# The last sequence's second half in its own banks: where the tail of one transformer layer is computed and sent

## The chip, the cores and the metric

The kernel runs on one NeuronCore of a Trainium2 chip. The metric is the device time of one execution in microseconds (us); the time of a version is the median over several executions. TensorE, VectorE, ScalarE, GpSimd (POOL) and SyncE each have a queue of their own and are ordered only by semaphores.

## The reference

One layer over 16 sequences of 256 tokens and 128 features: attention of 16 heads of 8 features with rotary positions and a causal mask, then a mixture of eight experts with one expert for each token, each followed by a residual addition and a normalisation.

```python
x = _layernorm(x + attention(x, wq, bq, wk, bk, wv, bv, wo, bo))
x = _layernorm(x + ffn(x, wg, W, b))
# _layernorm(x) = (x - mean) / sqrt(var + 1e-5), over the 128 features
# ffn: probs = softmax(x @ wg), expert = argmax(probs); a token counts if fewer
#      than 512 tokens before it took the same expert; out = prob * (x @ W[e].T + b[e])
```

## The kernel before

The work is a software pipeline over sequences. A loop over steps s runs on every engine (all_steps); in step s the stages of several sequences stand side by side: n = s+2 (projections and rotation), a = s+1 and b = s (operands and row maxima of the scores), c = s-1 (scores, exponentials, product with V), d = s-2 (output projection, first norm, routing, experts) and e = s-3 (second norm and output). Each step has 14 numbered slots, and each engine's order in a step is written out by hand by slot. Steps go from -2 to B+1 = 17; with B = 16 sequences the last step, 17, holds only d = 15 and e = 14, and behind it comes a short epilogue for e = 15. In the last step and the epilogue there are no other sequences' scores beside the chain.

In a step, what bears on the change is this. TensorE: the output projection of d (line 900, into ps_n), transposes of x1 (906), routing logits (948), locations (956 to 962), and the experts in two halves of 128 tokens, t = 0 in slot 12 and t = 1 in slot 13 (function experts, lines 814 to 816 through three, and 834). A half writes two PSUM banks, ps_m, one for experts 0 to 3 and one for 4 to 7: four matmuls of 512 columns for each bank, eight in all. The fourth adds a large negative number to all experts but the chosen one, so that VectorE finds the token's output as a maximum over the eight experts (select, line 668, into y_sel). Half 1 waits in TensorE's queue for moe_taken, which select of half 0 increments, since both halves use ps_m.

VectorE: in slot 3 it takes the second half of sequence e (select), in slot 4 it makes z2 = y_sel * gate_kept + x1 of e (add_experts, line 661, one instruction a half) and behind that z1 = projection + x_bias of d (line 706) with its statistics (norm_stats, lines 649 and 653, into st1 and mv1), in slot 5 x1 of d (line 712, two instructions, one a half), in slot 11 the statistics of z2.

GpSimd: inverse_deviation (line 356 adds epsilon, line 358 raises to the power -0.5) turns mv1 into rs1 and mv2 into rs2. output(e) does that for the second norm, waits until the store before has landed, scales z2 into y_out (line 367, one instruction a half) and sends both halves as one DMA from its own queue (line 372, semaphore stored). At the end it waits for all 16 stores.

SyncE's queue issues the loads and the traffic of rotated parts through DRAM (plain_parts, line 323, 64 KB each). Its last DMA is the load of x_res of sequence 15 (line 315), which GpSimd adds to a bias into x_bias (line 400).

After the last step the epilogue is: on VectorE select(15, 1), add_experts(15), norm_stats of z2; on GpSimd output(15).

Of the kernel before, what the change touches and what calls it, by code (L numbers as in the profile page):

```python
# [27 lines left out]
B, S, D = 16, 256, 128  # L28
# [60 lines left out]
def layer_kernel(nc, x, wq, bq, wk, bk, wv, bv, wo, bo, wg, W, b, const, expert_rows, out):  # L89
    f32, fr, bf = mybir.dt.float32, mybir.dt.float32r, mybir.dt.bfloat16  # L90
    ALU, ACT, AX = mybir.AluOpType, mybir.ActivationFunctionType, mybir.AxisListType
    x_t = x.rearrange("b (n p) d -> b p n d", p=128)
    out_t = out.rearrange("b (n p) d -> b p n d", p=128)
# [4 lines left out]
    with ExitStack() as ctx:  # L98
# [3 lines left out]
        def pb(name, shape):  # L102
            return ctx.enter_context(nc.psum_tensor(name, shape, f32))
# [28 lines left out]
        route_rows = sb("route_rows", [128, E * 128], fr)  # L132
# [30 lines left out]
        x_res, x_bias = sb("x_res", [128, 2, 128]), sb("x_bias", [128, 2, 128])  # L163
# [11 lines left out]
        kept, n_kept, gate_kept = sb("kept", [128, 2, E]), sb("n_kept", [128, 2]), sb("gate_kept", [128, 2])  # L175
        route = sb("route", [128, S], fr)

        ps_a = [pb(f"ps_a{i}", [128, 512]) for i in range(2)]
        ps_b = [pb(f"ps_b{i}", [128, 512]) for i in range(2)]
        ps_pv = pb("ps_pv", [128, 2, S])  # L180
        ps_m = pb("ps_m", [128, 2, 512])
        ps_n = pb("ps_n", [128, 512])
# [5 lines left out]
        names = []  # L188
# [18 lines left out]
                    gate_done rank_done first_done chosen_done seen_done loc_ready route_done nkept_done gk_done  # L207
                    moe_ready moe_taken""".split()

        names += """z2_done st2_done mv2_done ve2_done rs2_done out_done""".split()  # L210
        s_ = {name: sem(name) for name in names}

        def after(eng, name, t, per=1, k=0):

            n = t * per + k
            if isinstance(n, int):
                n = min(n, B * per)
                if n <= 0:
                    return
            eng.wait_ge(s_[name], n)  # L220
# [5 lines left out]
        def of_seq(v, t):  # L226

            return v[t] if isinstance(t, int) else v[bass.ds(t, 1)].squeeze(0)
# [18 lines left out]
        def by_half(t):  # L247

            return t[:, :, :].rearrange("p j (half m) -> p j half m", half=2)

        def is_step(s, which):

            return isinstance(s, int) and s == which

        def has(t):
            return not isinstance(t, int) or 0 <= t < B
# [9 lines left out]
        def all_steps(eng, step):  # L266


            for s in range(-2, 3):
                step(s, s % 2, lambda o: (s + o) // 2)  # L270
            with eng.Fori(0, (B - 6) // 2) as u:
                for k in range(2):
                    step(u * 2 + (3 + k), (3 + k) % 2, lambda o: u + (3 + k + o) // 2)
            for s in range(B - 3, B + 2):
                step(s, s % 2, lambda o: (s + o) // 2)
# [5 lines left out]
        def _(sp):  # L281
# [64 lines left out]
                    load_b(b, p)  # L346

            all_steps(sp, step)

        @block.gpsimd  # L350
        def _(pool):
# [8 lines left out]
            def output(e):  # L360

                inverse_deviation(mv2, rs2, 2, e)
                after(pool, "rs2_done", e, 1, 1)
                after(pool, "stored", e, 16)
                pool.nop(nofuse=True)
                for t in range(2):
                    last = pool.tensor_scalar(y_out[:, t, :], z2[:, t, :], mv2[:, t, 0:1], rs2[:, t:t + 1],  # L367
                                              ALU.subtract, ALU.mult)
                last.then_inc(s_["out_done"], 1)
                after(pool, "out_done", e, 1, 1)  # L370
                pool.nop(nofuse=True)
                pool.dma_start(of_seq(out_t, e), y_out[:, :, :]).then_inc(s_["stored"], 16)
# [87 lines left out]
                    output(e)  # L460

            all_steps(pool, step)
            output(B - 1)
            pool.wait_ge(s_["stored"], 16 * B)

        @block.scalar
        def _(act):
# [100 lines left out]
        def _(dve):  # L568
# [76 lines left out]
            def norm_stats(z, st, mv, n, d):  # L645

                after(dve, f"z{n}_done", d, 1, 1)
                for t in range(2):
                    dve.bn_stats(st[:, t, :], z[:, t, :]).then_inc(s_[f"st{n}_done"], 1)
                for t in range(2):  # L650
                    after(dve, f"st{n}_done", d, 2, t + 1)
                    dve.nop(nofuse=True)
                    dve.bn_aggr(mv[:, t, :], st[:, t, :]).then_inc(s_[f"mv{n}_done"], 1)  # L653

            def add_experts(e):

                after(dve, "out_done", e)
                for t in range(2):
                    after(dve, "moe_taken", e, 2, t + 1)
                    after(dve, "gk_done", e, 1, 1)  # L660
                    last = dve.scalar_tensor_tensor(out=z2[:, t, :], in0=y_sel[:, t, :], scalar=gate_kept[:, t:t + 1],
                                                    in1=x1[:, t, :], op0=ALU.mult, op1=ALU.add)
                last.then_inc(s_["z2_done"], 1)

            def select(d, t):

                after(dve, "moe_ready", d, 2, t + 1)
                dve.tensor_reduce(y_sel[:, t, :], ps_m[:, :, :].rearrange("p a (e f) -> p f (a e)", e=4),  # L668
                                  AX.X, ALU.max).then_inc(s_["moe_taken"], 1)

            def step(s, p, half):
                n, a, b, c, d, e = s + 2, s + 1, s, s - 1, s - 2, s - 3
                for slot in range(SLOTS):
# [21 lines left out]
                    if slot == 2 and has(d):  # L695
# [1 line left out]
                        after(dve, "y_ready", d)  # L697
                        after(dve, "den_done", d, 2, 2)
                        dve.tensor_tensor(attn[:, :], weighted[:, :], inv_den[:, :], ALU.mult).then_inc(s_["normed"], 1)
                    if slot == 4 and has(e):  # L700
                        add_experts(e)
                    if slot == 4 and has(d):

                        after(dve, "y_ready", d, 1, 1)
# [2 lines left out]
                                          x_bias[:, :, :], ALU.add).then_inc(s_["z1_done"], 1)  # L707
                        norm_stats(z1, st1, mv1, 1, d)
                    if slot == 5 and has(d):
                        after(dve, "rs1_done", d, 1, 1)  # L710
                        for t in range(2):
                            dve.tensor_scalar(x1[:, t, :], z1[:, t, :], mv1[:, t, 0:1], rs1[:, t:t + 1],  # L712
                                              ALU.subtract, ALU.mult).then_inc(s_["x1_done"], 1)
# [63 lines left out]

            all_steps(dve, step)
            select(B - 1, 1)
            add_experts(B - 1)  # L780
            norm_stats(z2, st2, mv2, 2, B - 1)

        @block.tensor
        def _(pe):
# [33 lines left out]
            def experts(d, n, t):  # L818

                if t == 0:  # L820
                    if has(n):
                        after(pe, "roped", n, 1, 1)
                    else:
                        after(pe, "vrows_done", d + 2, 1, 1)
                else:
                    after(pe, "moe_taken", d, 2, 1)
                for h in range(2):
                    o = ps_m[:, h, :].rearrange("p (e f) -> p e f", e=4)
                    tok = slice(128 * t, 128 * t + 128)
                    three(o, (x1t_hi[:, tok], x1t_lo[:, tok]), (we_hi[:, 4 * h:4 * h + 4, :], we_lo[:, 4 * h:4 * h + 4, :]),  # L830
                          True, False)
                    if h == 0:
                        after(pe, "route_done", d, 1, 1)
                    mm = pe.matmul(ps_m[:, h, :], route[:, tok], route_rows[:, 512 * h:512 * h + 512],  # L834
                                   start=False, stop=True, skip_group_check=True)
                mm.then_inc(s_["moe_ready"], 1)

# [181 lines left out]
```

## Time and profile before

| what | us |
|---|---|
| three runs | 463.35, 462.91, 461.01 |
| median | 462.91 |
| the profiled execution, its own time | 461.8 |
| its span in the trace | 460.1 |
| TensorE busy in the span | 410.3 |

The span goes from the first to the last instruction of the core; the execution's own time is 1.7 us more. The granted TensorE clock was 0.971 of full in the mean. The rows below are from that execution, and their times count from the span's start. The names PE, PEld, DVE, ACT, POOL and SP are TensorE's matmuls, its weight loads, VectorE, ScalarE, GpSimd and SyncE; a q behind a name is the engine's queue or sequencer. In the chain of waits, a piece begins where the piece before it released it, so that an instruction's piece can be shorter than the instruction. "issue" is time in which an engine waited for nothing that the profile shows.

### The profile page before, as it was taken

The numbers are of one execution on the slowest core, as the hardware profiler recorded it, in microseconds if no ns is written. First come the engines' busy times: TensorE is split into PE (matmuls) and PEld (weight loads), VectorE is DVE, ScalarE is ACT, GpSimd is POOL, SyncE is SP. The second block draws the span as 40 slices with busy tenths as digits, with TensorE's granted clock in tenths as the row PEclk, the third lists the DMA queues.
The fourth block names the chain that finished last, engine by engine and source line by source line (L and its number), as shares of the span: only waits on it lengthen the run. The fifth ranks groups of instructions, "written<-read, shape, count | busy, mean of one in ns | idle before, by whom it ended". The sixth has DMA issues, their size and how long they took to land. (4 is left out here: it accounts for less than half of the span.)

```text
span 460.1 us, 10441 instructions
## 1 busy us (share of the span) xinstructions
PE 410.3 (89%) x3270; PEld 359.2 (78%) x3270; DVE 317.8 (69%) x809; ACT 170.4 (37%) x375; POOL 207.8 (45%) x384
## 2 busy tenths in 40 slices
PE   3548598999999999999999999999999999999651
PEld 2426497989899888989898989898989888988540
DVE  8395444668686877877787878786868686855542
ACT  5152234343343434433434343434344343344100
POOL 6562324342545455463646463636363545151333
PEclk9999798999999999999999999999999999999957
DMA  5299872857669594939393939496678677610000
GB/s 139 51 156 157 131 111 61 134 88 133 95 122 123 122 115 113 130 93 151 84 160 88 147 84 144 90 147 92 144 99 147 82 134 97 76 33 1 11 0 24
DMA packets 145587, 47.29 MB, mean 103 GB/s; under 512 B 104333, under 2 KB 141841, under 8 KB 145562
## 3 DMA queue, kind: packets, MB, share of 16 engines
q1 hardware_dynamic: 139610, 42.52, 58.2%
q10 hardware_dynamic: 5184, 2.36, 2.7%
q0 software_dynamic: 768, 2.10, 1.6%
q8 instruction: 13, 0.21, 0.2%
q14 instruction: 12, 0.10, 0.1%
HBM read 30.70 MB, written 14.68 MB: 99 GB/s over the span
## 5 line engine op out<-in xcount | busy, mean ns | idle before, releaser
L881 PE MATMUL ps_pv<-probs,v_diag 128*128 128x64 f32 (+3 forms) x1024 | 190.0, 321 | 3.1 <-ACT probs L517 2.7
L881 PEld LDWEIGHTS ps_pv<-probs,v_diag 128*128 128x128 f32 x1024 | 148.0, 192 | 12.0 <-ACT probs L517 6.2
L517 ACT ACTIVATE probs<-ps_b 128x512 f32<-128x512 f32 (+1 forms) x176 | 97.5, 559 | 149.3 <-PE ps_b L845 145.0
L682 DVE TENSOR_REDUCE row_max<-ps_a 128x2 f32<-128x512 f32 (+3 forms) x176 | 108.3, 631 | 22.3 <-PE ps_a L845 21.9
L869 PE MATMUL ps_a<-k_plain,q_diag 128*128 128x64 bf16 (+3 forms) x512 | 67.2, 242 | 7.7 <-DMA q_diag<-plain_parts 4.4
L860 PE MATMUL ps_b<-q_plain,k_diag 128*128 128x64 bf16 (+3 forms) x512 | 65.6, 236 | 3.4 <-DMA q_plain<-max_rows 3.4
L668 DVE TENSOR_REDUCE y_sel<-ps_m 128x128 f32<-128x1024 f32 x32 | 39.0, 1219 | 18.7 <-PE ps_m L834 18.7
L869 PEld LDWEIGHTS ps_a<-k_plain,q_diag 128*128 128x128 bf16 x512 | 35.1, 101 | 20.2 <-issue 8.6
L419 POOL COPY v_diag<-v_rows 64x128 f32<-64x128 f32 x64 | 18.4, 288 | 68.6 <-PE ps_pv L881 33.9
L860 PEld LDWEIGHTS ps_b<-q_plain,k_diag 128*128 128x128 bf16 x512 | 36.3, 98 | 11.5 <-issue 4.2
L845 PE MATMUL ps_a<-mask_a_bf,ident_bf 128*128 128x128 bf16 (+2 forms) x176 | 44.6, 254 | 0.0
L845 PE MATMUL ps_b<-mask_b_bf,ident_bf 128*128 128x128 bf16 (+2 forms) x176 | 43.3, 246 | 0.0
L692 DVE RECIPROCAL inv_den<-sums 128x128 f32<-128x128 f32 x16 | 15.2, 953 | 37.0 <-ACT sums L483 37.0
L356 POOL TENSOR_SCALAR rs<-mv 128x2 f32<-128x2 f32 x32 | 7.3, 229 | 73.4 <-DVE mv L653 73.4
L451 POOL TENSOR_TENSOR rot_rest<-rot 128x512 f32<-128x512 f32 x16 | 18.5, 1154 | 38.0 <-ACT rot L561 38.0
L814 PE MATMUL ps_m<-we_hi,x1t_hi 128*128 128x512 f32 x64 | 28.6, 448 | 1.3 <-DVE y_sel L668 1.3
L753 DVE SCALAR_TENSOR_TENSOR rot_cs<-ps_m,bias_cols,cst 128x256 f32<-128x256 f32 x32 | 15.3, 479 | 19.5 <-PE ps_m L816 19.5
L448 POOL TENSOR_TENSOR rot<-rot_cs 128x512 f32<-128x512 f32 x16 | 20.6, 1288 | 14.2 <-DVE rot_cs L756 12.5
L367 POOL TENSOR_SCALAR y_out<-z,mv,rs 128x128 f32<-128x128 f32 x32 | 25.4, 797 | 3.6 <-POOL rs L358 3.6
L815 PE MATMUL ps_m<-we_lo,x1t_hi 128*128 128x512 f32 x64 | 25.8, 403 | 0.0
L816 PE MATMUL ps_m<-we_hi,x1t_lo 128*128 128x512 f32 x64 | 25.7, 402 | 0.0
L834 PE MATMUL ps_m<-route_rows,route 128*128 128x512 f32 x64 | 25.5, 399 | 0.0
(142 smaller groups left out, 716.3 us busy)
## 6 DMA issues: line engine op xcount, KB each, us to landing
plain_parts<-rot SPq DMA_DIRECT2D x180, 64.0 KB, 2.0
k_plain<-plain_parts SPq DMA_DIRECT2D x16, 384.0 KB, 3.8
q_diag<-plain_parts SPq DMA_DIRECT2D x32, 192.0 KB, 5.3
q_plain<-plain_parts SPq DMA_DIRECT2D x16, 384.0 KB, 6.2
k_diag<-plain_parts SPq DMA_DIRECT2D x32, 192.0 KB, 6.6
x_in<-in_L_attn_x_dram SPq DMA_DIRECT2D x16, 128.0 KB, 5.9
x_res<-in_L_attn_x_dram SPq DMA_DIRECT2D x16, 128.0 KB, 3.0
out_dram<-y_out POOLq DMA_DIRECT2D x16, 128.0 KB, 2.5
```

Of the source, the lines that this page charges most:

```text
L367: last = pool.tensor_scalar(y_out[:, t, :], z2[:, t, :], mv2[:, t, 0:1], rs2[:, t:t + 1], ALU.subtract, ALU.mult)
L517: act.activation(probs[:, k % PR, 0:cols], ps_b[k % 2][:, 0:cols], ACT.Exp, scale=SCALE)\
L668: dve.tensor_reduce(y_sel[:, t, :], ps_m[:, :, :].rearrange("p a (e f) -> p f (a e)", e=4), AX.X, ALU.max).then_inc(s_["moe_taken"], 1)
L682: last = dve.tensor_reduce(row_max[:, NBLK - 1 - j, groups[0]:groups[-1] + 1], scores[:, :, col:col + width(j)], AX.X, ALU.max)
L814: pe.matmul(out, sh, mh, start=start, stop=False, skip_group_check=True)
L815: pe.matmul(out, sh, ml, start=False, stop=False, skip_group_check=True)
L816: return pe.matmul(out, sl, mh, start=False, stop=stop, skip_group_check=True)
L834: mm = pe.matmul(ps_m[:, h, :], route[:, tok], route_rows[:, 512 * h:512 * h + 512], start=False, stop=True, skip_group_check=True)
L845: return pe.matmul(v, ident_bf[:, :], rows, start=False, stop=True, skip_group_check=True)
L860: pe.matmul(ps_b[k % 2][:, col:col + width(j)], diag_block(k_diag[q], g, j), q_plain[q][:, g, BLK * j:S], start=(i == 0), stop=False, skip ...
L869: pe.matmul(ps_a[k % 2][:, col:col + width(j)], diag_block(q_diag[at], g, NBLK - 1 - j), k_plain[at][:, g, 0:width(j)], start=(i == 0), st ...
L881: mm = pe.matmul(ps_pv[:, g // 4, BLK * j:S], v_diag[q][:, j, 128 * g:128 * g + 128], probs[:, k % PR, col:col + width(j)], start=(j == 0 ...
```

## The change

Only the last sequences are treated differently; the loop is as it was. The scores' four PSUM banks become one tensor ps_ab, cut into ps_a and ps_b as before. For sequence 15 the second half of the experts goes to the first two of these banks (expert_bank) and no longer waits for moe_taken. In step 17 the two additions of sequence 14 move from slot 4 to slot 5, behind z1 and its statistics, and x1 of sequence 15 waits for them, since they read x1 of sequence 14. For sequence 15 the second norm uses z1, st1, mv1 and rs1 in place of z2, st2, mv2 and rs2, and doesn't wait for the output of sequence 14. VectorE in place of GpSimd scales, from z1 into x_bias, one half at a time, and SyncE sends each half when it is done. GpSimd at the end waits for 15 stores and the two halves.

```diff
--- before.py
+++ after.py
@@ -175,8 +175,8 @@
         kept, n_kept, gate_kept = sb("kept", [128, 2, E]), sb("n_kept", [128, 2]), sb("gate_kept", [128, 2])
         route = sb("route", [128, S], fr)
 
-        ps_a = [pb(f"ps_a{i}", [128, 512]) for i in range(2)]
-        ps_b = [pb(f"ps_b{i}", [128, 512]) for i in range(2)]
+        ps_ab = pb("ps_ab", [128, 4, 512])
+        ps_a, ps_b = [ps_ab[:, i, :] for i in range(2)], [ps_ab[:, i, :] for i in range(2, 4)]
         ps_pv = pb("ps_pv", [128, 2, S])
         ps_m = pb("ps_m", [128, 2, 512])
         ps_n = pb("ps_n", [128, 512])
@@ -207,7 +207,7 @@
                     gate_done rank_done first_done chosen_done seen_done loc_ready route_done nkept_done gk_done
                     moe_ready moe_taken""".split()
 
-        names += """z2_done st2_done mv2_done ve2_done rs2_done out_done""".split()
+        names += """z2_done st2_done mv2_done ve2_done rs2_done out_done last_done last_stored""".split()
         s_ = {name: sem(name) for name in names}
 
         def after(eng, name, t, per=1, k=0):
@@ -247,6 +247,10 @@
         def by_half(t):
 
             return t[:, :, :].rearrange("p j (half m) -> p j half m", half=2)
+
+        def expert_bank(d, t):
+
+            return ps_ab[:, 0:2, :] if t == 1 and is_step(d, B - 1) else ps_m
 
         def is_step(s, which):
 
@@ -346,6 +350,10 @@
                     load_b(b, p)
 
             all_steps(sp, step)
+            for t in range(2):
+                sp.wait_ge(s_["last_done"], t + 1)
+                sp.nop(nofuse=True)
+                sp.dma_start(of_seq(out_t, B - 1)[:, t, :], x_bias[:, t, :]).then_inc(s_["last_stored"], 16)
 
         @block.gpsimd
         def _(pool):
@@ -460,8 +468,9 @@
                     output(e)
 
             all_steps(pool, step)
-            output(B - 1)
-            pool.wait_ge(s_["stored"], 16 * B)
+            inverse_deviation(mv1, rs1, 2, B - 1)
+            pool.wait_ge(s_["stored"], 16 * (B - 1))
+            pool.wait_ge(s_["last_stored"], 2 * 16)
 
         @block.scalar
         def _(act):
@@ -652,9 +661,10 @@
                     dve.nop(nofuse=True)
                     dve.bn_aggr(mv[:, t, :], st[:, t, :]).then_inc(s_[f"mv{n}_done"], 1)
 
-            def add_experts(e):
-
-                after(dve, "out_done", e)
+            def add_experts(e, z2):
+
+                if z2 is not z1:
+                    after(dve, "out_done", e)
                 for t in range(2):
                     after(dve, "moe_taken", e, 2, t + 1)
                     after(dve, "gk_done", e, 1, 1)
@@ -665,7 +675,7 @@
             def select(d, t):
 
                 after(dve, "moe_ready", d, 2, t + 1)
-                dve.tensor_reduce(y_sel[:, t, :], ps_m[:, :, :].rearrange("p a (e f) -> p f (a e)", e=4),
+                dve.tensor_reduce(y_sel[:, t, :], expert_bank(d, t)[:, :, :].rearrange("p a (e f) -> p f (a e)", e=4),
                                   AX.X, ALU.max).then_inc(s_["moe_taken"], 1)
 
             def step(s, p, half):
@@ -697,8 +707,8 @@
                         after(dve, "y_ready", d)
                         after(dve, "den_done", d, 2, 2)
                         dve.tensor_tensor(attn[:, :], weighted[:, :], inv_den[:, :], ALU.mult).then_inc(s_["normed"], 1)
-                    if slot == 4 and has(e):
-                        add_experts(e)
+                    if slot == (5 if is_step(s, B + 1) else 4) and has(e):
+                        add_experts(e, z2)
                     if slot == 4 and has(d):
 
                         after(dve, "y_ready", d, 1, 1)
@@ -707,6 +717,8 @@
                                           x_bias[:, :, :], ALU.add).then_inc(s_["z1_done"], 1)
                         norm_stats(z1, st1, mv1, 1, d)
                     if slot == 5 and has(d):
+                        if is_step(s, B + 1):
+                            after(dve, "z2_done", e, 1, 1)
                         after(dve, "rs1_done", d, 1, 1)
                         for t in range(2):
                             dve.tensor_scalar(x1[:, t, :], z1[:, t, :], mv1[:, t, 0:1], rs1[:, t:t + 1],
@@ -777,8 +789,12 @@
 
             all_steps(dve, step)
             select(B - 1, 1)
-            add_experts(B - 1)
-            norm_stats(z2, st2, mv2, 2, B - 1)
+            add_experts(B - 1, z1)
+            norm_stats(z1, st1, mv1, 2, B - 1)
+            after(dve, "rs2_done", B - 1, 1, 1)
+            for t in range(2):
+                dve.tensor_scalar(x_bias[:, t, :], z1[:, t, :], mv1[:, t, 0:1], rs1[:, t:t + 1],
+                                  ALU.subtract, ALU.mult).then_inc(s_["last_done"], 1)
 
         @block.tensor
         def _(pe):
@@ -822,16 +838,16 @@
                         after(pe, "roped", n, 1, 1)
                     else:
                         after(pe, "vrows_done", d + 2, 1, 1)
-                else:
+                elif not is_step(d, B - 1):
                     after(pe, "moe_taken", d, 2, 1)
                 for h in range(2):
-                    o = ps_m[:, h, :].rearrange("p (e f) -> p e f", e=4)
+                    o = expert_bank(d, t)[:, h, :].rearrange("p (e f) -> p e f", e=4)
                     tok = slice(128 * t, 128 * t + 128)
                     three(o, (x1t_hi[:, tok], x1t_lo[:, tok]), (we_hi[:, 4 * h:4 * h + 4, :], we_lo[:, 4 * h:4 * h + 4, :]),
                           True, False)
                     if h == 0:
                         after(pe, "route_done", d, 1, 1)
-                    mm = pe.matmul(ps_m[:, h, :], route[:, tok], route_rows[:, 512 * h:512 * h + 512],
+                    mm = pe.matmul(expert_bank(d, t)[:, h, :], route[:, tok], route_rows[:, 512 * h:512 * h + 512],
                                    start=False, stop=True, skip_group_check=True)
                 mm.then_inc(s_["moe_ready"], 1)
```

## Rows read from the trace of the kernel before

**Rows 1.** The page, engines: busy us, share of the span, instructions.

```profile
PE 410.3 (89%) x3270; PEld 359.2 (78%) x3270; DVE 317.8 (69%) x809; ACT 170.4 (37%) x375; POOL 207.8 (45%) x384
```

**Rows 2.** Stretches of ten us: busy of each engine, granted clock, DMA.

```profile
420.00:430.00 10.00, 9.99 (x88) 9.12 (x87) 4.52 (x19) 3.15 (x7) 3.50 (x7) 1.00 0.01 2
430.00:440.00 10.00, 3.84 (x19) 2.56 (x18) 5.97 (x14) 1.90 (x5) 1.93 (x4) 0.84 0.04 13
```

**Rows 3.** Chain of waits, 430 to 461 us: start us, length us, what.

```profile
433.46 1.22 DVE y_sel L668
...
435.20 0.34 DVE z L706
...
436.16 0.19 DVE mv L653
...
436.51 0.24 POOL rs L356
...
436.82 0.73 POOL rs L358
...
437.57 0.61 DVE x L712 x2
...
442.97 0.43 PE ps_m L814
...
445.95 0.44 PE ps_m L834
...
446.42 1.23 DVE y_sel L668
...
447.70 0.50 PE ps_m L814
448.19 0.23 PE ps_m L815
...
449.58 0.25 PE ps_m L834
...
452.88 0.73 POOL rs L358
...
453.81 1.59 POOL y_out L367 x2
...
455.94 0.82 POOL out_dram L372
```

**Rows 4.** TensorE in half-us stretches: length, busy, granted clock, DMA share, GB/s.

```profile
436.50:437.00 0.50, 0.00 (x0) 0.78 0.00 0
...
447.00:447.50 0.50, 0.00 (x0) 0.98 0.00 0
```

**Rows 5.** Line 774: duration ns min/median/max, first and last start.

```profile
L774 DVE TENSOR_TENSOR gate_kept<-n_kept,gate x16: 160/644/727, 93.9 to 443.7; 128x2 f32<-128x2 f32 x16
```

**Rows 6.** Timeline around 336 us: start us, length us, engine, line, what.

```profile
336.07 1.28 POOL L448 TENSOR_TENSOR rot<-rot_cs 128x512 f32<-128x512 f32 x1 [0.16 <-POOL seen L444]
...
336.65 0.71 DVE L774 TENSOR_TENSOR gate_kept<-n_kept,gate 128x2 f32<-128x2 f32 x1
```

**Rows 7.** DMA issues from 450 us on: KB, us from issue to landing.

```profile
out_dram<-y_out POOLq DMA_DIRECT2D x1, 128.0 KB, 2.4
```

**Rows 8.** Line 315's loads from 380 us on: issue ns, us to landing.

```profile
L315 SPq DMA_DIRECT2D x_res<-in_L_attn_x_dram x3: 390/2805/3222, 379.2 to 411.3; - x3
...
DMA to landing us min/median/max: 2.2/6.6/6.7
```

**Rows 9.** Line 323's writes to DRAM, whole trace: issue ns, us to landing.

```profile
L323 SPq DMA_DIRECT2D plain_parts<-rot x180: 539/547/937, 19.7 to 371.2; - x180
...
DMA to landing us min/median/max: 2.0/2.0/3.3
```

**Rows 10.** GpSimd's sequencer at the end of the program (L98), ns.

```profile
L98 POOLq DRAIN  x1: 1382/1382/1382, 458.5 to 458.5; - x1
```

**Rows 11.** GpSimd's sequencer at the start of the program (L1006), ns.

```profile
L1006 POOLq DRAIN  x1: 169/169/169, 0.4 to 0.4; - x1
```

## Prediction

> **What bounds the kernel now.** I read the page first. TensorE is busy 89% of the span [rows 1], so over the body of the kernel a change must relieve TensorE. The edits all lie in the last steps, so next I read the stretches of ten us: TensorE is full until 430 us and then falls to 38% [rows 2]. From there on it is one sequence's chain of dependent small steps. The third view, the chain of waits, is the one that prices this change. The reader is to see that from 433.46 us on it runs through every operation that the diff touches: the reduction of sequence 14's second half, its two additions, the normalisation of sequence 15, both halves of its experts, and the tail with inverse deviation, scaling and store [rows 3]. Whatever is taken out of this chain moves the end one for one, as long as nothing else becomes late. The fourth view is the granted clock in half-us stretches, since the second part of the change puts matmuls where TensorE now idles at half clock [rows 4].
>
> **Part 1, the two additions of sequence 14 go behind sequence 15's first norm.** At present VectorE ends the reduction at 434.68 and starts z1 at 435.20; between them stand the two additions of line 661, 0.52 us [rows 3]. The matmuls that z1 reads were done (the chain runs through the reduction, not through them), so z1 and all behind it could come 0.52 us earlier. The additions go between the norm statistics and x1. There VectorE now waits from 436.35 to 437.57 for the two GpSimd operations, lines 356 and 358 (starts 436.51 and 436.82) [rows 3]: 1.2 us of cover for 0.6 us of work. The added wait of x1 on z2_done holds nothing else back, for x1 is next in that queue anyway.
>
> But the cover is not free. Nowhere in the trace do the additions lie beside a GpSimd operation. The nearest row is line 774, a tiny product with both inputs in SBUF: it takes 0.16 us alone and 0.64 in the median, and in the instance shown it starts at 336.65 inside GpSimd's line 448 (336.07 for 1.28, to 337.35) and ends at 337.36 [rows 5, 6]. Such a VectorE operation stands still until GpSimd's is over. The additions have both inputs in SBUF too. They would start at once, 0.13 us or so before line 356, so here GpSimd may be the one that waits. Bounds: no collision, gain 0.52; GpSimd waits for both additions, or the second addition waits for line 358 and x1 for it, gain 0. I take 0.25, half way, since the collision is there [rows 6], but with the other engine first.
> The Trainium skill's page "SBUF — State Buffer", section "SBUF: two separate sides", says that VectorE with two SBUF inputs and GpSimd take a shared port pair in turn, whole instruction by whole instruction. The trace agrees [rows 6]. By that rule the gain of this part is near the low bound, by the cover alone at the high one; part 2 shows that the sum would be 0.14 us smaller or larger.
>
> **Part 2, the second half of the experts in other banks.** Now: the first half's eight matmuls stream from 442.97 to 446.39, 0.43 us apart; the reduction runs from 446.42 to 447.65; only then the second half starts at 447.70 and ends at 449.83, its matmuls 0.23 apart ((449.58 - 448.19)/6) after a first of 0.50 [rows 3]. With its own banks it starts right behind the first half. Only 1.31 us of idle time (446.39 to 447.70) and 0.27 of first-matmul fill can go. The 0.43 and 0.23 are the two levels of the clock: it fell to half (1.2 GHz) at about 436.8, when TensorE was mostly idle [rows 2], and was back at full (2.4 GHz) just after 447.0, behind the 3.4 us of the first half and during the wait for the reduction [rows 4]. So part of the second half now falls into the slow stretch. With part 1's 0.25, the stream starts at 442.72. A slow matmul takes (446.39 - 442.97)/8 = 0.4275. Up to 447.0, 4.28/0.4275 = 10.0 are done; the other 6.0 at 0.2325 take 1.39; end 448.39, against 449.83: 1.44 us for parts 1 and 2 together. Bounds: full clock from the first matmul of the second half, 446.14 + 8 x 0.2325 = 448.00, gain 1.83; half clock throughout, 446.14 + 8 x 0.4275 = 449.56, gain 0.27. With part 1 at its own bounds these become 2.1 and 0, and the middle case 1.58 (stream from 442.45) and 1.30 (from 442.97): of a shift ahead of the clock's rise only about half arrives behind it. I take the middle case, 1.44, as the rise stands there in the profile.
> The reduction of the first half (446.17 to 447.4) is then hidden behind the second half's matmuls, and the second reduction is not held up by it. It reads another pair of banks of the same size: 1.22 us as before. The last users of those banks, the maxima of sequence 15, come before its scores are exponentiated, long before 433, so that this wait costs nothing.
> The Trainium skill's page "TensorE: Matmul & The Clock Gate", section "Part 1: The HAM clock gate", says that activity releases the slower clock, and that the moment varies from run to run. The trace agrees on the two levels [rows 4]. By that rule the 1.44 is one draw out of the cases between the bounds.
>
> **Part 3, from the last matmul to the inverse deviation.** Same operations on z1, st1, mv1, rs1 in place of z2, st2, mv2, rs2. The chain from 449.83 to 453.61 stays: 3.78 us [rows 3], 0. Dropping the wait on out_done gives nothing: GpSimd's scaling of sequence 14 does not stand in the chain, the additions follow the reduction.
>
> **Part 4, scaling and store.** Now, counted from the end of rs (453.61): scaling starts at +0.20 and takes 1.59 on GpSimd, the DMA issue starts at +2.33 [rows 3] and the data land 2.4 later [rows 7], at 458.3 or +4.7. After: VectorE starts 0.03 after rs, two scalings in 0.61, as line 712 does on the same shape [rows 3]; the first is done at +0.37, SyncE issues at about +0.45. SyncE's queue is empty: its last DMA was the load of x_res at 411.3 [rows 8]. An issue of 64 KB from there costs 0.55 us, up to 0.94 [rows 9], so the second goes out at about +1.1, although its data is there at +0.64. Landing of 64 KB written to DRAM from SyncE: 2.0 in the median of 180, 3.3 at most [rows 9]. End at +3.1, against +4.7: gain 1.6. Bounds: issue 0.39, the least of the loads of x_res [rows 8], gain 1.8; landing 3.3, gain 0.3. The landing on an idle queue is the median's case, so I take 1.6. The tail of sequence 15 needs no more of GpSimd than lines 356 and 358.
> What follows the landing stays: GpSimd waits for last_stored in place of stored, then its DRAIN of 1.38 us (458.5 to 459.87) ends the span [rows 10]. That is the largest unpriced item. At the start of the span a DRAIN of GpSimd took 0.17 [rows 11], with no DMA of GpSimd's before it. After the change its last own DMA lies 9 us back. Bounds: 0 and -1.2; I take 0, since the DMA had landed before the DRAIN began in this trace also.
>
> **The sum.** 1.44 + 0 + 1.6 = 3.0 us. The profiled execution took 461.8 with a span of 460.1, so 458.8 with a span of 457.1. That execution lies 1.1 below the median of the three runs (462.91, from 461.01 to 463.35); the four average 462.3, which gives 459.3, and that is the forecast. A difference of 0.5% (2.3 us) is about what a measurement of this kernel can tell from none, and the forecast is not far beyond it. The rest of the kernel, up to 433 us, keeps the same instructions and the same banks: ps_a and ps_b are now one tensor cut in four.
>
> **The rivals.**
> A. The clock stays low through most of the second half. For: with no pause it starts 1.5 us sooner, nearer to the cold stretch. Against: more activity. Gain 0.27 + 1.6 = 1.9, time 460.4. Chance 0.17.
> B. The collision of part 1 eats all of it: line 356 begins behind both additions, at about 436.5 as now. For: the standstill of line 774 [rows 6]. Against: it is GpSimd that would have to stand, and short operations can take turns. Gain 1.30 + 1.6 = 2.9, time 459.4. Chance 0.15. (The page on SBUF named above would have it so.)
> C. GpSimd's closing DRAIN shrinks to 0.17. Gain 3.0 + 1.2 = 4.2, time 458.1. For: the start's DRAIN; against: above. Chance 0.12.
> D. The store in halves is no faster: a landing of 3.3 leaves 1.44 + 0.3 = 1.7, time 460.6. Chance 0.08.
> E. Slower: SyncE's queue gives late landings. Line 315, on the same queue, landed after 6.7 us at worst [rows 8]. Then the end is at +1.1 + 6.7 = +7.8 in place of +4.7, 3.1 lost, 1.44 won: 1.7 slower, 464.0. It decides from a landing of 5.0 us on. Against: those loads shared the queue with others' packets, and in the tail the DMA engines are nearly idle [rows 2]. Chance 0.04.
> F. The change does not do what it says: z1 or the second half is held by something that I don't see, and the net gain is under 1 us; 461.8. Chance 0.07.
>
> **How the numbers follow.** The forecast keeps 0.37. Faster by over 0.5%: forecast, B and C, 0.64, and a little of A and D by the spread of runs, 0.67. Within 0.5%: A, D and F, less that, 0.28. Slower: 0.05. The range takes in C below (458.1, less half a us for the spread) and A and D above, with the same allowance: 457.6 to 461.2. The likeliest case's own range is 458.4 to 460.0.
>
> **What would show it.** In the changed profile: z1 (line 706's successor) right behind the reduction, and the starts and durations of lines 356, 358 and 661 beside each other; sixteen expert matmuls without a gap, with the clock's rise somewhere in them and the last one's end some 1.4 us sooner; the second reduction starting at that end; two scalings of 0.34 on VectorE, two SyncE issues 0.6 apart, landing 2.0 after the second; GpSimd's DRAIN at 1.38. The prediction is wrong if the clock rises later than the end of the first half plus 2 us, if lines 356 and 358 start later than their cover allows, if landing takes over 3 us, or if the DRAIN changes.

## The result and the profile after

| | runs | median us | ratio to the kernel before |
|---|---|---|---|
| before | 4 | 462.54 (461.01 to 463.35) | |
| changed | 4 | 457.11 (456.55 to 457.47) | 0.9885 (0.9857 to 0.9914) |
| changed, measured again | 6 | 457.14 (456.32 to 459.51) | 0.9907 (0.9883 to 0.9932) |

The change wins 5.4 us where 3.0 to 3.2 were forecast, and ends half a us below the range. The profiled execution took 457.05 with a span of 455.4, so the two spans differ by 4.7. The second measurement gives 4.7 as well (461.87 for 19 executions of before). The ratios come from all executions of both kernels and differ a little from those of the medians. By the intervals of the ratios the gain lies between 4.0 and 6.6 us in the first measurement and between 3.1 and 5.4 in the second, so the first excludes the forecast 3.2 and the second has it at its edge.

The chain of waits of the changed kernel, in the tail (start us, length us, what). Lines 678, 716, 830, 832, 850, 366 and 796 answer to 668, 706, 814, 816, 834, 358 and 367 of [rows 3]:

```profile
433.17 1.22 DVE y_sel L678
434.38 0.34 DVE z L716
...
436.76 0.02 DVEq L220
...
442.22 0.43 PE ps_m L830
...
444.78 0.39 PE ps_m L832
445.17 0.24 PE ps_m L850
445.41 0.23 PE ps_ab L830
...
447.02 0.25 PE ps_ab L850
...
450.33 0.73 POOL rs L366
...
451.09 0.34 DVE x_bias L796
```

The reader sees z1 (434.38) right behind the reduction, the second half's matmuls (ps_ab, from 445.41) right behind the first half's, and the scaling (451.09) 0.03 us behind the inverse deviation. The granted clock of that trace in half-us stretches, as [rows 4]:

```profile
434.50:435.00 0.50, 0.00 (x0) 0.75 0.00 0
...
445.00:445.50 0.50, 0.50 (x4) 1.00 0.00 0
```

It fell at about 434.75 and rose at 445.0, within the first half: the seventh matmul of that half is the last slow one, and the whole second half runs at 0.23 us a matmul.

The timeline of the additions in their new place and of the last stores, then the stores' landing (KB, us from issue) and GpSimd's closing DRAIN, which answer to [rows 7] and [rows 10]:

```profile
435.48 0.61 DVE L671 SCALAR_TENSOR_TENSOR z<-y_sel,gate_kept,x 128x128 f32<-128x128 f32 x2
435.69 0.23 POOL L364 TENSOR_SCALAR rs<-mv 128x2 f32<-128x2 f32 x1 [4.98 <-DVE mv L662]
436.00 0.72 POOL L366 TENSOR_TENSOR rs<-rs,minus_half 128x2 f32<-128x2 f32 x1
...
451.09 0.60 DVE L796 TENSOR_SCALAR x_bias<-z,mv,rs 128x128 f32<-128x128 f32 x2 [1.24 <-POOL rs L366]
451.50 0.84 SPq L356 DMA_DIRECT2D out_dram<-x_bias  x2
```

```profile
out_dram<-x_bias SPq DMA_DIRECT2D x2, 64.0 KB, 1.6
```

```profile
L98 POOLq DRAIN  x1: 1301/1301/1301, 453.8 to 453.8; - x1
```

The two additions (line 671) and the two GpSimd operations behind the statistics lie side by side, none late or long against [rows 3]. Line 364 falls wholly inside the additions, line 366 overlaps them by only 0.09 us. The two stores take 0.84 us to issue, 0.37 each and a gap. With both traces cut at the same five places, the stages are, in us:

| stage | before | changed | won | forecast |
|---|---|---|---|---|
| body, up to the reduction of sequence 14 | 433.46 | 433.17 | 0.29 | 0 |
| from there to the first matmul of the experts | 9.51 | 9.05 | 0.46 | 0.25 |
| the experts' sixteen matmuls with the pause | 6.86 | 5.05 | 1.81 | 1.19 |
| last matmul to the end of the inverse deviation | 3.78 | 3.79 | 0 | 0 |
| from there to GpSimd's DRAIN | 4.9 | 2.8 | 2.1 | 1.6 |
| DRAIN to the end | 1.6 | 1.5 | 0.1 | 0 |

Of the 0.53 us by which z1 comes earlier, 0.46 reach the experts: x1 starts 0.10 us behind line 366 in place of 0.02, because VectorE passes the added wait on z2_done there (DVEq, line 220, above).

### The profile page after: what moved, and what is told of

Same layout as the page of the kernel before. It is cut to its first block and busy times, and to the rows that moved or that the text cites. A ratio compares the mean times of both kernels' runs of the same rounds, so it can differ in the third digit from the quotient of the medians.

```text
span 455.4 us, 10444 instructions
## 1 busy us (share of the span) xinstructions
PE 407.5 (89%) x3270; PEld 357.4 (78%) x3270; DVE 318.7 (70%) x811; ACT 170.4 (37%) x375; POOL 205.4 (45%) x381
## 5 line engine op out<-in xcount | busy, mean ns | idle before, releaser
L526 ACT ACTIVATE probs<-ps_ab 128x512 f32<-128x512 f32 (+1 forms) x176 | 97.5, 559 | 151.5 <-PE ps_ab L861 147.6
L692 DVE TENSOR_REDUCE row_max<-ps_ab 128x2 f32<-128x512 f32 (+3 forms) x176 | 108.4, 631 | 24.6 <-PE ps_ab L861 24.2
L885 PE MATMUL ps_ab<-k_plain,q_diag 128*128 128x64 bf16 (+3 forms) x512 | 67.7, 244 | 10.2 <-DMA q_diag<-plain_parts 5.0
L876 PE MATMUL ps_ab<-q_plain,k_diag 128*128 128x64 bf16 (+3 forms) x512 | 65.6, 236 | 2.8 <-DMA q_plain<-max_rows 2.8
L885 PEld LDWEIGHTS ps_ab<-k_plain,q_diag 128*128 128x128 bf16 x512 | 35.2, 101 | 22.9 <-issue 12.5
L678 DVE TENSOR_REDUCE y_sel<-ps_m 128x128 f32<-128x1024 f32 x31 | 37.8, 1220 | 16.2 <-PE ps_m L850 16.2
L876 PEld LDWEIGHTS ps_ab<-q_plain,k_diag 128*128 128x128 bf16 x512 | 36.3, 99 | 11.0 <-issue 3.7
L861 PE MATMUL ps_ab<-mask_a_bf,ident_bf 128*128 128x128 bf16 (+2 forms) x176 | 44.7, 254 | 0.0
L861 PE MATMUL ps_ab<-mask_b_bf,ident_bf 128*128 128x128 bf16 (+2 forms) x176 | 43.3, 246 | 0.0
L375 POOL TENSOR_SCALAR y_out<-z,mv,rs 128x128 f32<-128x128 f32 x30 | 23.7, 795 | 3.4 <-POOL rs L366 3.4
```

Of the source, the lines that this page charges most:

```text
L526: act.activation(probs[:, k % PR, 0:cols], ps_b[k % 2][:, 0:cols], ACT.Exp, scale=SCALE)\
L678: dve.tensor_reduce(y_sel[:, t, :], expert_bank(d, t)[:, :, :].rearrange("p a (e f) -> p f (a e)", e=4), AX.X, ALU.max).then_inc(s_["moe_t ...
L692: last = dve.tensor_reduce(row_max[:, NBLK - 1 - j, groups[0]:groups[-1] + 1], scores[:, :, col:col + width(j)], AX.X, ALU.max)
L861: return pe.matmul(v, ident_bf[:, :], rows, start=False, stop=True, skip_group_check=True)
L876: pe.matmul(ps_b[k % 2][:, col:col + width(j)], diag_block(k_diag[q], g, j), q_plain[q][:, g, BLK * j:S], start=(i == 0), stop=False, skip ...
L885: pe.matmul(ps_a[k % 2][:, col:col + width(j)], diag_block(q_diag[at], g, NBLK - 1 - j), k_plain[at][:, g, 0:width(j)], start=(i == 0), st ...
```

## The experiments

The stages of the profiled executions, worked out from their chains of waits in the same way (us; the body is left out, as it differs between executions of the same kernel):

| kernel | to the experts | experts | inverse deviation to DRAIN |
|---|---|---|---|
| before, first profile | 9.51 | 6.86 | 4.9 |
| before, second profile | 9.50 | 8.53 | 4.9 |
| additions alone | 9.05 | 8.41 | 4.9 |
| banks alone | 9.51 | 4.83 | 4.9 |
| tail alone | 9.51 | 8.53 | 2.8 |
| changed | 9.05 | 5.05 | 2.8 |
| changed, again | 8.82 | 4.98 | 2.8 |
| changed, with four additions | 9.20 | 5.81 | 2.8 |
| changed, with one store | 9.06 | 5.01 | 2.8 |
| before with fillers | 9.13 | 5.94 | 4.9 |
| changed with fillers | 8.18 | 3.88 | 2.8 |
| changed with more fillers | 8.18 | 3.89 | 2.8 |

In the second profile of the changed kernel the clock fell only at 437.4, in place of 434.75, so the two transposes of x1 took 0.47 us and not 0.70; hence its 8.82.

**1. The additions alone.**

```diff
-                    if slot == 4 and has(e):
+                    if slot == (5 if is_step(s, B + 1) else 4) and has(e):
                         add_experts(e)
...
                     if slot == 5 and has(d):
+                        if is_step(s, B + 1):
+                            after(dve, "z2_done", e, 1, 1)
```

> Only the two additions of sequence 14 are moved behind sequence 15's statistics; banks and tail are those of the kernel before. Theory 1 (no collision: the two engines' reads do not meet): z1 starts right behind the reduction, lines 356 and 358 keep their distance to the statistics and their 0.23 and 0.72 us, the time falls by 0.45 to 0.5 us. Theory 2 (shared port, as the prediction took half of it): line 356 or 358 is late or long, gain 0 to 0.25.

Measured: 461.38 (459.68 to 464.68, 12 runs), ratio 1.000 (0.9974 to 1.0026). An effect of 0.5 us is inside that interval, so the time can't confirm it; the trace does. Four of the twelve executions, the profiled one among them, took 464.1 to 464.7, above all 59 of before (463.9 at most), and the others 459.7 to 461.7. In the profiled one the reduction of sequence 14 came late, at 434.75, ahead of the edit's place; why is not shown. Its chain of waits:

```profile
434.75 1.22 DVE y_sel L668
435.96 0.34 DVE z L706
...
443.80 0.43 PE ps_m L816
...
448.53 0.80 PE ps_m L816
449.33 0.43 PE ps_m L817
```

From the reduction to z1 it is 1.21 us in place of 1.74, to the experts' first matmul 9.05 in place of 9.51: theory 1. But the second half (from 448.53) is at 0.43 us a matmul, and the experts take 8.41 in place of 6.86. The edit isn't needed for that: experiment 4 finds the same in the kernel before.

**2. The banks alone.** The edit is ps_ab, expert_bank and the wait on moe_taken, as in the change.

> Only the second half of sequence 15's experts goes to other banks. Theory 1 (the pause is what is won, the clock decides how much): no gap between the sixteen matmuls, gain 1.0 to 1.9 us, by where the clock rises: from the start of the first half to the end of the second 6.9 us before, 4.9 to 5.9 now. Theory 2 (without the pause the clock comes back reliably earlier, so the time of before had an additional loss in other executions): gain over 2 us in the median, and the spread of the runs is smaller than that of before.

Measured: 459.66 (457.31 to 460.70, 8 runs), ratio 0.9939 (0.9914 to 0.9964), 2.2 us in the medians. The chain of waits, where the clock rises and where the second half begins and ends:

```profile
443.91 0.43 PE ps_m L818
...
446.04 0.36 PE ps_m L819
...
446.87 0.23 PE ps_ab L818
...
448.49 0.25 PE ps_ab L838
```

Sixteen matmuls without a gap, 4.83 us: 2.03 less than in the first profile of before. The gain is over 2 us in the median, as theory 2 has it, but the interval (1.7 to 4.0) doesn't exclude theory 1, and the spread of the runs (3.4, of 8 executions) is hardly smaller than that of before (3.7, of 19). Which of the two is right stays open.

**3. The tail alone.** The change without expert_bank and without the move.

> Only the last norm's buffers, its scaling on VectorE and the store by SyncE in halves; additions and banks as before. Theory 1 (what the changed kernel's trace showed holds alone too): store lands 2.5 to 2.6 us after the inverse deviation in place of 4.7, gain 2.1 to 2.2 us. Theory 2 (the prediction's 1.6 was right for an ordinary landing and the trace had a lucky one): landing 2.0 after the issue, gain 1.6.

Measured: 459.65 (457.54 to 461.34, 6 runs), ratio 0.9937 (0.9913 to 0.9962), 2.2 us in the medians. The two stores and the DRAIN:

```profile
455.78 0.84 SPq L356 DMA_DIRECT2D out_dram<-x_bias  x2
```

```profile
L98 POOLq DRAIN  x1: 1301/1301/1301, 458.1 to 458.1; - x1
```

The inverse deviation ends at 455.33; the stores are issued and land as in the changed kernel (1.6 us), and it is 2.8 in place of 4.9 us to the DRAIN: theory 1.

All three parts together, once more:

> The changed kernel once more, beside the parts on the same chip. If the parts add, its gain is the sum of the three single gains within 0.5 us, 4.4 to 5.4 us. If one part opens room for another (the clock), it is more than the sum by over 0.5 us.

Measured: 457.14 (456.32 to 459.51, 6 runs), 4.7 us under before (461.87). The single gains are 0.5, 2.2 and 2.2 us by the medians, 4.9 together. By the medians the parts add. The ratios give 0, 2.8 and 2.9 us singly, 5.7 together, against 4.3 for the whole change, each with about 1.2 us to either side, so that the sum is known only within a us or two. That one part opens something for another is not seen.

**4. The kernel before, profiled once more.**

> The kernel before once more, for a second profile and more times. Theory 1 (in part of its executions the second half of the experts runs at half clock): the second half takes 3.4 us from the first reduction's start in some profiles and 5.0 to 5.1 in others; its times spread over 3 us or more. Theory 2 (both other kernels with the pause were slow by their own edits): 3.4 again, and a spread that comes from the body.

Measured: 461.07 (459.83 to 463.34, 10 runs), ratio 0.9994 (0.9972 to 1.0017). Its chain of waits, and its granted clock in half-us stretches:

```profile
433.01 1.22 DVE y_sel L668
...
442.51 0.43 PE ps_m L814
...
445.97 1.24 DVE y_sel L668
...
447.25 0.80 PE ps_m L814
448.04 0.43 PE ps_m L815
...
450.60 0.44 PE ps_m L834
...
451.07 0.07 DVE y_sel L668
```

```profile
446.50:447.00 0.50, 0.00 (x0) 0.50 0.00 0
...
451.00:451.50 0.50, 0.03 (x1) 0.88 0.00 0
```

The same kernel, but the clock rises at 451.1 in place of 447.0, and the second half (447.25 to 451.04) runs at 0.43 us a matmul. The experts take 8.53 us in place of 6.86. Theory 1: with the pause, the kernel before has both outcomes, 1.67 us apart. Its copies with the additions or the tail alone have one profile each, and both show the slow one (8.41 and 8.53); so of the four profiles with the pause three are slow, and the forecast was built on the fourth. How often each outcome comes can't be told from four. This execution took 463.0. In the profiles with the new banks the clock rose from 2.3 to 4.4 us behind the first matmul, so that the experts took 4.83 to 5.81 us and never the whole 6.8 of sixteen slow ones.

**5. The clock held up.** In step 17, matmuls of 512 columns that nobody reads go into TensorE's idle times: 13 behind the output projection, 2 behind the transposes, 5 behind the logits.

```diff
+            def fill(count):
+                for _ in range(count):
+                    pe.matmul(ps_ab[:, 3, :], ident_bf[:, :], q_plain[0][:, 0:2, :], start=True, stop=True,
+                              skip_group_check=True)
...
                         mm.then_inc(s_["y_ready"], 1)
+                        if is_step(s, B + 1):
+                            fill(13)
```

> The changed kernel with 20 matmuls of 512 columns more in step 17 (13 behind the output projection, 2 behind the transposes, 5 behind the logits) into an idle bank; nobody reads them. Theory 1 (the clock sets what is left of the experts' time): the granted clock stays at full from 433 us on, the first half's matmuls come 0.23 us apart in place of 0.43, the sixteen take 3.7 us in place of 5.1 to 5.3, transposes and logits are shorter too; the time falls by 1.5 to 2.5 us against the changed kernel. Theory 2 (the slow matmuls are slow for what they read, not for the clock): 0 or a loss, as the fillers stand in the queue ahead of the chain.

Measured: 454.42 (453.55 to 456.77, 6 runs), ratio to before 0.9838 (0.9808 to 0.9868), 7.9 us under before and beyond the interval of the changed kernel. No version that was run has a lower median. Five-us stretches of TensorE (busy, granted clock), and the chain of waits:

```profile
430.00:435.00 5.00, 3.64 (x19) 1.00 0.01 2
435.00:440.00 5.00, 3.58 (x18) 1.00 0.00 0
440.00:445.00 5.00, 4.34 (x21) 1.00 0.00 0
```

```profile
432.33 1.22 DVE y_sel L678
...
440.51 0.24 PE ps_m L830
...
441.21 0.38 PE ps_m L856
...
442.52 0.23 PE ps_ab L830
...
444.14 0.25 PE ps_ab L856
```

The clock is at 1.00 until the experts are done, and they take 3.88 us: all sixteen matmuls at full clock, with a wait of 0.15 us for the routing. Theory 1.

The kernel before with the same fillers:

> The kernel before with the same 20 matmuls. Theory 1: both halves run at full clock in every execution, 1.9 us each with the pause between, so that it wins 1.6 us (first half) against the profiled execution of before and up to 1.6 more against executions in which the second half was slow too: 2 to 3 us in the median. The difference between this kernel and the changed one with fillers is then what the clock has no part in: 0.5 for the additions, 1.3 + 0.3 for the pause, 2.15 for the tail, 4.2 us together. Theory 2: as for the other kernel, 0 or a loss.

Measured: 458.99 (457.64 to 459.29, 6 runs), ratio 0.9925 (0.9900 to 0.9950), 3.4 us under before. Its granted clock shows that 20 fillers don't always hold it:

```profile
439.00:439.50 0.50, 0.50 (x3) 0.69 0.00 0
...
442.50:443.00 0.50, 0.50 (x4) 0.90 0.00 0
```

It was low from 439.2 to 442.6, against theory 1, which had both halves at full clock in every execution. The five fillers behind the logits then ran slow as well: from the logits to the locations it was 1.87 us, where the changed kernel with fillers has 1.40. The experts still take 5.94 us, 0.9 to 2.6 less than without fillers. Against the changed kernel with fillers the difference is 4.6 us in the medians, where 4.2 were worked out.

The changed kernel with 27 fillers:

> As the changed kernel with fillers, with 27 of them (4 more ahead of the output projection, 14, 3 and 6 in the three other pauses). Theory 1 (the clock fell inside the tail in some executions with 20 fillers, as in the trace of the kernel before with fillers): fewer executions over 455.5 us, median at or up to 0.5 us below that with 20. Theory 2 (20 are enough, more only delay the chain): median 0.2 to 0.5 us higher.

Measured: 454.73 (453.39 to 455.54, 5 runs), ratio 0.9853 (0.9832 to 0.9873). The tail is as long as with 20 fillers (both 20.1 us from the reduction of sequence 14 to the end), and the medians can't be told apart; one execution of five was over 455.5 (455.54), where with 20 it was one of six (456.77). Which theory is right stays open.

**6. VectorE against GpSimd in the cover.** Two more additions of the same form stand ahead of the two moved ones.

```diff
+                        if is_step(s, B + 1):
+                            for t in range(2):
+                                dve.scalar_tensor_tensor(out=weighted[:, 128 * t:128 * t + 128], in0=y_sel[:, t, :],
+                                                         scalar=gate_kept[:, t:t + 1], in1=x1[:, t, :],
+                                                         op0=ALU.mult, op1=ALU.add)
                         add_experts(e, z2)
```

> The changed kernel with two more additions of the same form ahead of the two moved ones (into a buffer that nobody reads any more), so that VectorE works with two SBUF inputs during all of lines 356 and 358 of before (364 and 366 now). Theory 1 (no standstill at this size): the four start 0.26 to 0.27 us apart, the two GpSimd operations keep their starts at 0.16 and 0.47 after the statistics and their 0.23 and 0.72 us. Theory 2 (they take turns, and the two additions had only missed each other): one of the two engines is held, an addition lasts over 0.5 us or a GpSimd operation starts over 0.2 late, and x1 is later by as much as exceeds the cover.

Measured: 458.58 for one execution. Its timeline (start, length, engine, line), to be held against that of the changed kernel above:

```profile
436.05 0.58 DVE L713 SCALAR_TENSOR_TENSOR weighted<-y_sel,gate_kept,x 128x128 f32<-128x128 f32 x2
436.31 0.23 POOL L364 TENSOR_SCALAR rs<-mv 128x2 f32<-128x2 f32 x1 [4.99 <-DVE mv L662]
436.56 0.60 DVE L671 SCALAR_TENSOR_TENSOR z<-y_sel,gate_kept,x 128x128 f32<-128x128 f32 x2
436.62 0.86 POOL L366 TENSOR_TENSOR rs<-rs,minus_half 128x2 f32<-128x2 f32 x1
```

And line 671 alone:

```profile
L671 DVE SCALAR_TENSOR_TENSOR z<-y_sel,gate_kept,x x2: 339/340/340, 436.6 to 436.8; 128x128 f32<-128x128 f32 x2
```

With four, the additions keep their pace, line 364 its 0.23 us, and line 366 takes 0.86 in place of the 0.72 that it has again at 451.85 in the same execution. So there is a collision, but it costs GpSimd 0.14 us, with two more additions than the change has. Neither theory is right as put: no standstill, but one operation longer by a fifth. The last addition began at 436.8, inside line 366 (436.62 to 437.48), and took its 0.34 us all the same. So it isn't only that VectorE came first: here GpSimd's operation was under way, as line 448 was in [rows 6], and nothing stood still. That is one execution.

**7. What in the tail is won.** One store by SyncE behind both scalings:

```diff
-            for t in range(2):
-                sp.wait_ge(s_["last_done"], t + 1)
-                sp.nop(nofuse=True)
-                sp.dma_start(of_seq(out_t, B - 1)[:, t, :], x_bias[:, t, :]).then_inc(s_["last_stored"], 16)
+            sp.wait_ge(s_["last_done"], 2)
+            sp.nop(nofuse=True)
+            sp.dma_start(of_seq(out_t, B - 1), x_bias[:, :, :]).then_inc(s_["last_stored"], 16)
```

> The changed kernel with one store of 128 KB by SyncE behind both scalings in place of two. Theory 1 (the start on SyncE and the short landing are what is won, the halves hardly matter): the store is issued 0.7 us after the inverse deviation and lands after 1.7 to 1.9, so that the end is 0.1 us earlier to 0.1 later than with halves. Theory 2 (halves overlap): it lands 2.0 or more after its issue, the end is 0.2 to 0.4 later.

Measured: 457.62 for one execution. Timeline, and the landing:

```profile
450.87 0.72 POOL L365 TENSOR_TENSOR rs<-rs,minus_half 128x2 f32<-128x2 f32 x1
...
452.30 0.39 SPq L355 DMA_DIRECT2D out_dram<-x_bias  x1
```

```profile
out_dram<-x_bias SPq DMA_DIRECT2D x1, 128.0 KB, 1.9
```

The store is issued at +0.71 behind the inverse deviation (451.59) and lands 1.9 later; with halves the second is issued at +0.91 and lands 1.6 later. From the inverse deviation to the DRAIN it is 2.81 against 2.77 us: theory 1, the halves are worth nothing that one execution of each could show.

The same single store from GpSimd's queue, behind VectorE's scaling:

> The changed kernel, scaled by VectorE, but sent by GpSimd in one store of 128 KB. Theory 1 (scaling and queue each give a part): the issue comes 0.7 + 0.5 us after the inverse deviation (0.5 for GpSimd's start of a store, as in the kernel before), lands 2.3 to 2.4 later: store landed at +3.6, against +2.6 with SyncE and +4.7 before; so 1.1 of the 2.15 us is the scaling and 1.05 the queue. Theory 2 (GpSimd's lateness came from its own scaling just before): issue 0.1 after the scaling, landed at +3.1.

Measured: 457.95 for one execution. Timeline, and the landing:

```profile
450.25 0.72 POOL L362 TENSOR_TENSOR rs<-rs,minus_half 128x2 f32<-128x2 f32 x1
...
452.15 0.78 POOL L471 DMA_DIRECT2D out_dram<-x_bias  x1 [1.18 <-issue]
```

```profile
out_dram<-x_bias POOLq DMA_DIRECT2D x1, 128.0 KB, 2.3
```

Issued at +1.18, landed 2.3 later at +3.5, the DRAIN starts at +3.7. Of the 2.1 us, 1.2 come from the scaling on VectorE (4.9 to 3.7) and 0.9 from SyncE's queue (3.7 to 2.8). Theory 1.

## Why the prediction was wrong

The direction, the places and the order of the parts were right, and parts 1, 2 and 4 each gave more than their terms of the sum. The mechanism held; what failed were three sizes, and two of them, the experts and the store, were each short by about 0.6 us. Rivals A to F did not occur: the clock came back earlier, not later; the DRAIN took 1.30 us, not 0.17; and the stores landed early.

**Part 1** was sized at 0.25 and measured 0.53 up to z1, 0.46 up to the experts. The step that failed is the carrying over of line 774's standstill [rows 5, 6] to the additions. There the GpSimd operation ran over 512 elements for 1.28 us; lines 356 and 358 work on two. Experiment 6 gives 0.14 us as the cost of a longer overlap, and in the change itself nothing got longer, so the bound 0.52 was nearly the right value; the added wait, which the text put at nothing, costs the 0.07 between it and 0.46. Experiment 6 also rules out that only the order of the two engines differs. That GpSimd's small operand is what spares VectorE is argued, not shown. The trace agrees less with the Trainium skill's page "SBUF — State Buffer", section "SBUF: two separate sides", than I made it. In [rows 6] the standstill of line 774 shows as a longer record, 0.71 us in place of 0.16. By turns of whole instructions line 364, which began inside the first addition, or the second addition, which began inside line 364, would be long in the same way; they took 0.23 and 0.34 us, as alone. Whether the reads themselves take turns within these times is not shown.

**Part 2** was sized at 1.19 (1.44 with part 1) and measured 1.81. The step that failed is the middle case: it kept the rise of the clock at the profile's 447.0, 4.3 us behind the first matmul. In the changed kernel it came 2.8 us behind it (445.0 - 442.22), and over the profiles with new banks 2.3 to 4.4 behind: the last of these, with four additions, took 5.81 us, near the 5.67 of the forecast. It was a draw, as the text said, but the bounds were too narrow for it on both sides. On the side of the change, they let the clock rise with the first matmul of the second half at the earliest, which gives 2.1 us for parts 1 and 2 together. The measured 2.27 lie beyond, because the clock rose within the first half. On the side of before, they took the 6.86 us of its profile as the time to be beaten, and the second profile has 8.53. Between 8.53 and 5.05 the same edit wins 3.5 us. So a forecast from one profile of before could have been off by 1.7 us for this alone, and the range had no such term. That the measured stage came as near to the forecast as 0.6 us is in part luck: the profile of before happened to be the fast outcome.

**Part 3** was right: 3.79 us against 3.78, and dropping the wait on out_done gave nothing.

**Part 4** was sized at 1.6 and measured 2.1. Two durations of [rows 9] did not hold for this store: the issue took 0.37 us, not 0.55 (the lower bound 0.39 of [rows 8] was right), and the landing 1.6, although the least of the 180 was 2.0. The bounds of the landing came from one kind of write, and so there was none below 2.0. Why this store lands sooner than those writes is not shown. The DRAIN was right, 1.30 against 1.38, though GpSimd's own last store was 6 us back and not 9.

**The sum.** By stages the tail won 4.45 us in place of 3.0: 0.2 from part 1, 0.6 from part 2, 0.6 from part 4 with the DRAIN. The body gave another 0.29, which nothing in the change explains: over the traces of this case the reduction of sequence 14 starts anywhere from 432.2 to 434.8. The spans account for 4.7 of the 5.4; the rest comes of medians of four executions: the median of all 59 executions of before is 461.95, that of all ten of the changed kernel 457.11, 4.8 us. The first profile of before, at 461.8, was close to its kernel's median after all, and moving the forecast up by half a us towards 462.3 took it further from the measured time. What spreads the body's start and the times of before (459.7 to 463.9), beyond the 1.7 us of the experts, stays open.

## What to carry to other kernels

In a tail of dependent steps, add up the chain and then ask for each term whether its duration is a constant or a draw: here matmuls behind a quiet stretch took 0.23 or 0.43 us by the moment at which the clock rose, and one profile shows one draw. A pause in TensorE ahead of its last work can cost more than its own length: here it was 1.3 us long, and removing it won 2.2 by the medians. Matmuls that nobody reads, put into such pauses, won 2.7 us, at least as much as any single edit of the change. For a last output, the engine that scales and the queue that sends are each worth about a us; cutting the store in halves showed no gain.

## What the runs showed of the hardware

- The same kernel's second half ran at 0.23 us a matmul in one execution and at 0.43 in another, by a rise of the granted clock at 447.0 or 451.1.
- The first matmul behind the pause took 0.50 us at full clock and 0.80 at half clock, 0.27 and 0.37 more than those behind it.
- A 64 KB store from SyncE landed 1.6 us after its issue, one of 128 KB 1.9, and one of 128 KB from GpSimd 2.3.
- GpSimd's closing DRAIN took 1.38 us where it had sent the last store and 1.30 where it had not, 6 us behind its last store: the store hardly matters for it.
- VectorE's additions with two inputs in SBUF and GpSimd's two-element operations ran side by side. With two additions nothing got longer; with four the second GpSimd operation did, by 0.14 us.
